# Cross-attention and a mixture of experts: token tiles in groups inside the last attention turns, the token list built from lanes, outputs back in 2 KB rows

## Reference

```python
x = x + attn(layernorm(x), ctx, ctx, mask, Wq, bq, Wk, bk, Wv, bv, Wo, bo)
flat = layernorm(x).reshape(-1, 256)                      # 1792 rows
probs = softmax(flat @ router_w)                          # 8 experts
topk_w, topk_idx = top_k(probs, 2); topk_w /= topk_w.sum(-1)
h = silu(einsum('td,edf->etf', flat, w1))                 # 256 -> 512
y = einsum('etf,efd->etd', h, w2)                         # 512 -> 256
x = x + sum of topk_w * y over a token's two experts
```

## Time and profile before

| | |
|---|---|
| median of 3 executions | 522.26 us (521.93 to 522.46) |
| profiled execution, its own time | 520.47 us |
| its span, first to last instruction | 518.3 us |
| mean granted TensorE clock | 0.896 of 2.4 GHz |
| busy: PE, DVE, ACT, POOL | 424.2 (82%), 348.9 (67%), 262.6 (51%), 189.3 (37%) us |
| chain that ended last | PE 74%, DVE 9%, issue 5%, DMA 4%, ACT 4% |
| moved by DMA | 70.08 MB, mean 135 GB/s; fullest slice 393 GB/s |

### The profile page before, as it was taken

How to read it: one execution, slowest core, us unless ns; L and a number is a source line. 1 busy time by engine, 2 the same in 40 slices (tenths; PEclk the granted TensorE clock), 3 DMA queues, 4 the chain that set the end, 5 groups by cost and what they waited for, 6 DMA issues and landing times.

```text
span 518.3 us, 10586 instructions
## 1 busy us (share of the span) xinstructions
PE 424.2 (82%) x4151; PEld 391.1 (75%) x4151; DVE 348.9 (67%) x743; ACT 262.6 (51%) x338; POOL 189.3 (37%) x162
## 2 busy tenths in 40 slices
PE   2666689999999999999996758445799999999800
PEld 2454489999999999999885657345799999999800
DVE  2776557788788788877871296474667667777427
ACT  3230245666666566666555204101877777777500
POOL 8270462222222222222100430007277777776410
PEclk9796779999999999999999687655999999999965
DMA  7949658676666677775604398002022222221158
GB/s 179 220 145 282 181 149 161 136 143 148 134 146 136 147 152 151 151 151 124 122 4 145 103 393 307 10 1 81 32 82 83 92 82 90 84 91 63 52 166 289
DMA packets 60609, 70.08 MB, mean 135 GB/s; under 512 B 19313, under 2 KB 55681, under 8 KB 60561
## 3 DMA queue, kind: packets, MB, share of 16 engines
q1 hardware_dynamic: 48224, 48.18, 39.8%
q0 software_dynamic: 4032, 11.02, 6.3%
q10 hardware_dynamic: 8304, 10.23, 5.6%
HBM read 35.64 MB, written 15.04 MB: 98 GB/s over the span
## 4 chain that ended last, share of the span: by engine, by line
PE 74%; DVE 9%; issue 5%; DMA 4%; ACT 4%; POOL 2%; SPq 1%; POOLq 0%; DVEq 0%; ACTq 0%
PE ps L1268 39%; PE ps L1329 11%; PE ps L1344 9%; PE ps L1358 8%; PE ps L1558 2%; ACT probs L678 2%; DMA y_back<-y_rows 2%; PE ps L1371 1%; SPq L477 1%; DVE x_rows_sb L927 1%; PE ps L1548 1%; DVE neg_max L880 1%; PE ps L1508 1%; DVE stats L916 1%; PE ps L1381 1%
## 5 line engine op out<-in xcount | busy, mean ns | idle before, releaser
L880 DVE TENSOR_REDUCE neg_max<-ps 112x1 f32<-112x376 f32 x256 | 133.7, 545 | 39.1 <-PE ps L1329 34.0
L678 ACT ACTIVATE probs<-ps 125x1344 f32<-125x1344 f32 x64 | 82.7, 1292 | 42.4 <-PE ps L1344 36.5
L1329 PE MATMUL ps<-k_stack,q_stack 98*112 98x376 f32 x256 | 89.2, 383 | 10.1 <-issue 6.0
L508 POOL TENSOR_TENSOR k_lo<-k_f,k_hi 128x752 fp32r<-128x752 f32 x16 | 28.8, 1802 | 139.2 <-ACT k_hi L652 136.7
L617 POOL DMA_INDIRECT y_rows<-y_out,slot_of_row x42 | 53.2, 1266 | 37.2 <-ACT y_out L814 30.8
L609 POOL DMA_INDIRECT rows<-xn_rows,token_of_row x42 | 42.9, 1021 | 61.2 <-DVE token_of_row L1142 47.5
L1329 PEld LDWEIGHTS ps<-k_stack,q_stack 98*112 98x112 f32 x256 | 45.7, 181 | 24.1 <-DVE neg_max L880 13.4
L1344 PE MATMUL ps<-q_stack,k_stack 100*125 100x224 f32 x384 | 53.6, 276 | 3.3 <-ACT probs L678 3.0
L1344 PEld LDWEIGHTS ps<-q_stack,k_stack 100*125 100x125 f32 x384 | 51.2, 191 | 5.1 <-ACT probs L678 4.9
L1268 PE MATMUL ps<-w_hi,h_hi 128*128 128x256 f32 x168 | 49.0, 292 | 3.1 <-issue 1.6
L1268 PE MATMUL ps<-flat_t_hi,w_hi 128*128 128x256 f32 x168 | 48.8, 290 | 2.8 <-DVE flat_t_lo L1179 2.8
(11 more groups left out here) (189 smaller groups left out, 974.1 us busy)
## 6 DMA issues: line engine op xcount, KB each, us to landing
k_stack<-k_hi SPq DMA_DIRECT2D x64, 188.0 KB, 4.5
w_all<-w ACTq DMA_DIRECT2D x16, 512.0 KB, 8.4
k_stack<-k_lo SPq DMA_DIRECT2D x32, 188.0 KB, 5.4
ctx_raw<-ctx_t SPq DMA_DIRECT2D x32, 187.5 KB, 5.1
q_stack<-q_scratch SPq DMA_DIRECT2D x32, 168.0 KB
q_scratch<-q_hi SPq DMA_DIRECT2D x16, 224.0 KB, 3.1
y_back<-y_rows SPq DMA_DIRECT2D x14, 256.0 KB, 5.5
q_scratch<-q_lo SPq DMA_DIRECT2D x8, 224.0 KB, 2.9
```

What stands on the lines that cost most here:

```text
L508: pool.tensor_tensor(kl[:, :, :], kf[:, :, :], kh[:, :, :].bitcast(F32), ALU.subtract)\
L678: act.activation(pf[j % 2][:, :, :], ps[0:CT, BK_ST:BK_ST + KT, 0:4 * S], ACT.Exp).then_inc(pf_ready, 1)
L880: dve.tensor_reduce(neg_max[:, s:s + 1], ps[0:S, BK_MAX + s % 2, 0:CP], AX.X, ALU.max, negate=True).then_inc(max_read, 1)
L1329: pe.matmul(ps[0:S, BK_MAX + a, 0:CP], qs[b.ring][0:R_MAX, q, S * a:S * (a + 1)], ks[b.ring][0:R_MAX, q, :], start=True, stop=True).then_i ...
```

## The change

Token tiles are taken in units: six units of two tiles and two of one (`UNITS`). `project_output` of units 0 to 3 takes the place of the keys in turns 13 and 14, on PE, and `residual` that on DVE. x is loaded into `x2` ahead of SP's turn 10; POOL makes its constants and all seven bias adds after its turn 12, ahead of `key_low(15)`. The last batch's turn is written out on each engine, with units 4 to 7, transposes, routes and reads of logits woven in. Statistics and roots are taken in groups of 8, 4, 1 and 1 tiles: the first two by a power on POOL, which also normalises those tiles; the last two by Newton steps on DVE. The router's product is turned round: token tiles are stationary, 8 columns move, and the logits need no way back. The choice of experts, ranking and places are made for tiles 0 to 11 and then for tiles 12 and 13. The list: every expert has 14 lanes of 128 places, a place's lane doesn't depend on the other experts' counts, POOL writes each token's slot number in its lane (`lanes`), PE adds them up in 28 products (`fill_lanes`) and one product brings the lanes that are used to the blocks (`list_rows`). Spare rows read one row of zeros. `y_rows` keeps a token's two outputs side by side, so they come back in seven pieces of 512 KB. `weigh` comes after expert step 3. The weights are loaded by SP in two pieces, w1 after the last quad scores and w2 after the last `out_copy`, with the write-out of units 4 and 5 between and of 6 and 7 behind. Many buffers get other places in memory.

```diff
+UNITS = ((0, 2), (2, 2), (4, 2), (6, 2), (8, 2), (10, 2), (12, 1), (13, 1))
+GROUPS = ((0, 4), (4, 2), (6, 1), (7, 1))
+EARLY_NT = 12
...
@@ SP
             for b in range(B):
+                if b == 10:
+                    sp.wait_ge(qproj_done, 2 * NG)
+                    sp.dma_start(x2[:, :, :], x_tiles.rearrange("n p d -> p n d")).then_inc(x2_in, 16)
                 turn(Batch(0, b))
...
+            for u in range(0, 4):
+                write_rows(u)
+            sp.wait_ge(st_done, QUADS * B)
+            sp.dma_start(w1_all[:, :, :].rearrange("p e (k n) -> p (e k) n", k=KD),
+                         w1.rearrange("e k p n -> p (e k) n")).then_inc(w1_in, 16)
+            for u in range(4, 6):
+                write_rows(u)
+            sp.wait_ge(ot_ready, B)
...
+            for u in range(6, 8):
+                write_rows(u)
...
-                for c in range(TOP):
-                    sp.dma_start(y_back[c][:, 2 * g:2 * g + 2, :],
-                                 y_rows[c * T + g * TG:c * T + (g + 1) * TG, :].rearrange("(n p) d -> p n d", p=P))\
-                        .then_inc(y_in[g], 16)
+                sp.dma_start(y_back[:, 2 * g:2 * g + 2, :, :],
+                             y_rows[TOP + TOP * TG * g:TOP + TOP * TG * (g + 1), :]
+                             .rearrange("(n p c) d -> p n c d", p=P, c=TOP)).then_inc(y_in[g], 16)
@@ POOL
+            def roots(g):
...
+                pool.wait_ge(row_var_ready, g + 1)
+                pool.tensor_tensor(row_rstd[:, tiles], row_var[:, tiles], minus_half[:, tiles], ALU.pow)\
+                    .then_inc(row_rstd_ready, 1)
+            def normalise_rows(u):
+                pool.wait_ge(row_rstd_ready, 1 if u < 4 else 2)
+                if u >= RINGS:
+                    pool.wait_ge(ft_done, u - RINGS + 1)
+                    pool.wait_ge(xn_written[u % RINGS], 16)
...
+            def lanes(tiles, known):
+                pool.wait_ge(lanes_known, known)
+                for c in range(TOP):
+                    for n in range(tiles.start, tiles.stop):
+                        last = pool.tensor_scalar(placed[:, c, n, :], place_no[:, 0:ER], lane_of[:, c, n:n + 1],
+                                                  slot_no[:, c, n:n + 1], ALU.is_equal, ALU.mult)
+                last.then_inc(lanes_ready, 1)
+            for b in range(B + 1):
+                turn(Batch(0, b))
+                if b == B - 4:
+                    pool.wait_ge(x2_in, 16)
+                    pool.wait_ge(vo_bias_in, 16)
+                    constants()
+                    for g in range(NT // 2):
+                        add_bias(g)
+            roots(0)
+            for u in range(0, 4):
+                normalise_rows(u)
+            roots(1)
+            for u in range(4, 6):
+                normalise_rows(u)
+            lanes(slice(0, EARLY_NT), 1)
+            lanes(slice(EARLY_NT, NT), 2)
@@ ACT, last turn
+            out_copy(last.after(-1))
+            exps(last, 0)
+            exps(last, 1)
+            attn_high(last.after(-1))
+            exps(last, 2)
+            flat_high(0)
+            exps(last, 3)
+            flat_high(1)
+            flat_high(2)
+            out_copy(last)
+            flat_high(3)
+            flat_high(4)
+            attn_high(last)
+            flat_high(5)
...
@@ DVE: from row_vars(2) on
+            residual(6)
+            row_vars(2, row_stats(6))
+            normalise(last)
+            flat_low(3)
+            read_logits(3)
+            flat_low(4)
+            attn_low(last)
+            read_logits(4)
+            flat_low(5)
+            normalise_late(6)
+            read_logits(5)
+            residual(7)
+            row_vars(3, row_stats(7))
+            flat_low(6)
+            find_two(early_tiles, 6)
+            count_early()
+            normalise_late(7)
+            read_logits(6)
+            flat_low(7)
+            place_rows(early_tiles, BK_RANK, 1)
+            read_logits(7)
+            find_two(late_tiles, 8)
+            for c in range(TOP):
+                places_in_block(c, early_tiles)
+            place_rows(late_tiles, BK_LATE, 2)
+            for c in range(TOP):
+                places_in_block(c, late_tiles)
+            count_blocks()
+            blocks_of_lanes()
+            read_lanes()
+            list_tokens()
             plan_steps()
-            weigh()
             for n in range(-1, STEPS + 1):
                 expert_step(Batch(0, n))
+                if n == 3:
+                    weigh()
@@ PE
+            def route(u):
+                pe.wait_ge(fl_ready, u + 1)
+                for a in range(UNITS[u][1]):
+                    m = slice(a * P, (a + 1) * P)
+                    last = product(ps[:, BK_FLAT[u % 2], E * a:E * (a + 1)],
+                                   [(x[u % 2][:, k, m], w[:, k, :]) for k in range(KD)
+                                    for x, w in ((fh, rwh), (fh, rwl), (fl, rwh))])
+                last.then_inc(logits_done, 1)
...
+                    elif halves[-1] == KD - 1:
+                        project_output(2 * (b.n - B + 3) + t)
...
+            quad_outputs(last.after(-1), 2)
+            quad_outputs(last.after(-1), 3)
+            quad_scores(last, 0)
+            project_output(4)
+            out_transpose(last.after(-1))
+            quad_scores(last, 1)
+            quad_outputs(last, 0)
+            project_output(5)
+            attn_transpose(last.after(-1))
+            quad_scores(last, 2)
+            flat_transpose(0)
+            quad_outputs(last, 1)
+            flat_transpose(1)
+            quad_scores(last, 3)
+            route(0)
+            flat_transpose(2)
+            quad_outputs(last, 2)
+            route(1)
+            flat_transpose(3)
+            quad_outputs(last, 3)
+            project_output(6)
+            route(2)
+            flat_transpose(4)
+            out_transpose(last)
+            route(3)
+            flat_transpose(5)
+            attn_transpose(last)
+            route(4)
+            flat_transpose(6)
+            route(5)
+            project_output(7)
+            route(6)
+            rank_early()
+            flat_transpose(7)
+            route(7)
+            fill_lanes(slice(0, EARLY_NT))
+            rank_late()
+            fill_lanes(slice(EARLY_NT, NT))
             list_rows()
```

More of the change, by code:

```diff
@@ L146, in xattn_moe_kernel @@
         cursor["at"] = shared
+        x2 = sb("x2", [P, NT, D])
+        assert cursor["at"] <= q_end, "x2 lies where the transposed rows were"
+        cursor["at"] = q_end
+        attn_start = cursor["at"]
         expert_even = expert_buffers(0)
-        cursor["at"] = max(q_end, cursor["at"])
-        attn_start = cursor["at"]
+        late_start, cursor["at"] = cursor["at"], attn_start
+        placed = sb("placed", [P, TOP, NT, ER], F32R)
+        assert cursor["at"] <= attn_start + 6 * KD * CP * 4, "lanes lie where the context's parts were"
+        cursor["at"] = attn_start
         c_raw = [sb(f"ctx_raw{p}", [P, KD, CP]) for p in range(2)]
@@ L204, in xattn_moe_kernel @@
         assert cursor["at"] <= hidden_end, "the hidden rows lie where the transposed attention was"
-        cursor["at"] = hidden_at
-        is_place = sb("is_place", [P, TOP, NT, P], F32R)
-        is_its_block = sb("is_its_block", [P, TOP, NT, NB])
-        block_token = sb("block_token", [P, TOP, NT, NB], F32R)
-        assert cursor["at"] <= hidden_end, "the lists are made where the hidden rows come"
-        cursor["at"] = attn_start + 4 * NT * D
-        y_back = [sb(f"y_back{c}", [P, NT, D]) for c in range(TOP)]
+        cursor["at"] = late_start
@@ L238, in xattn_moe_kernel @@
+        is_place = sb("is_place", [P, TOP, NT, P], F32R)
+        assert cursor["at"] <= last_ring_end, "places lie where the last ring was"
+        cursor["at"] = last_ring_end
+        ones = sb("ones", [P, P], F32R)
+        earlier = sb("earlier", [P, P], F32R)
+        block_of_lane = sb("block_of_lane", [P, NB], F32R)
+        lane_tokens = sb("lane_tokens", [P, P], F32R)
+        slot_i = sb("slot_of_row", [P, NB], I32)
+        token_i = sb("token_of_row", [P, NB], I32)
         st2 = sb("stats2", [P, NT, 6])
@@ L988, in turn @@
                     keys(b.after(3), 0)
+                else:
+                    residual(2 * (b.n - B + 3) + 0)
                 if has(after):
@@ L992, in turn @@
                     keys(b.after(3), 1)
+                else:
+                    residual(2 * (b.n - B + 3) + 1)
                 if has(after):
@@ L1080, in find_second, with wide2 @@
-            def find_second():
-                step(dve.scalar_tensor_tensor(out=rest[:, :, :], in0=picked, scalar=-3.0e38,
-                                              in1=logits[:, :, :], op0=ALU.mult, op1=ALU.add))
-                step(dve.tensor_reduce(c2[:, :], rest[:, :, :], AX.X, ALU.max))
-                first_of(rest[:, :, :], c2, second)
-                dve.wait_ge(tri_set, 1)
```

(15 more changed lines are left out.)

640 lines of the change are left out of this document (333 added, 307 removed).

## The result

The changed kernel takes 544.07 us (median of 4 runs, 539.94 to 545.76) against 522.1 us before; two further executions of it took 537.50 and 542.70. The ratio, 1.038 with a 95% interval of 1.031 to 1.045, is taken from the means of all six and of the four before, without the longest of the six, which counts as a slow run. Forecast were 525.0 us and a range of 515 to 533: the direction was right, the size far off. The profiled execution took 539.94 us (span 538.1), before's 520.47 (span 518.3).

The account below looks back on a forecast made before the run. A serial chain from output projections to the first expert matmul (292.20 to 356.50 us) was taken as the bound. List +2.5 (including the earlier turns), weigh +1.2, rows back -1.0 gave +2.7: 522.26 to 525.0 us, range 515 to 533.

Parts of the forecast that it names:

- Part 1: Projections of tiles 0 to 7 in turns 13 and 14: +1.8 us a turn, +3.6 for both (0 to 5.7).
- Part 3: Constants and seven bias adds on POOL before the last key_low: +0.2 us, from 0 to 2.
- Part 2: Load of x, 1.8 MB, in turn 10 ahead of stacking batch 12's keys: +0.5 us, from 0 to 3.
- Part 4: Tail from last attention to the list, 24 POOL lanes at 0.30 us each: list complete +2.5 us (-1.9 to +3.8).
- the second rival: The rival "POOL sets the pace".
- POOL sets the pace: Tail: lanes at 0.46 (+3.8) and POOL standing still during DVE's comparisons (3.4): 532.2 us; chance 0.15.
- The clock stays up: Rival: the tail keeps PE at 2.4 GHz, 11.3 us less, 513.7 us, or 519.3 for half of that; chance 0.30.
- Part 5: Weigh in the fourth expert step, 3.1 us of delay on DVE: +1.2 us, from 0 to 1.8.
- Part 6: Outputs read back at the kernel's end in 2 KB rows, seven loads for fourteen: -1.0 us (-2.1 to 0).
- The power: Roots by power on POOL, no row to price it: hidden up to 3 us, at 4 costing 0.3.

Follow-up runs that it names:

- The pieces: Changed kernel with x loaded in seven pieces of two tiles, one ahead of each of turns 4 to 10, not one 1.8 MB load: 539.09 us.
- the load behind the stackings: Changed kernel with the single 1.8 MB load of x still in turn 10 but issued behind the stacking of batch 12: 544.17 us.
- with products added for it, and the lanes split: Changed kernel, x in pieces, power roots, late ranking and weights first, early lanes shared by DVE and POOL, plus unread products on PE: 509.8 us (515.61 without).
- the first set of added products: Changed kernel, x in pieces, all lanes on DVE, power roots, late ranking and weights first, plus 237 unread 256-column products on PE: 519.13 us (516.64 without).
- lanes on DVE: Changed kernel with all 28 lanes written on DVE and none on POOL: 536.25 us.
- places held: Changed kernel with DVE making the early places only once POOL's 24 early lanes are done: 545.28 us.
- powers: Changed kernel with the roots of the last two tiles taken by one power each on POOL, not 15 steps on DVE: 542.4 us.

## Why the prediction was wrong

**Part 1 was right.** 1.8 us for turn 13 and 3.6 for both. Part 3 was right: key_low of batch 15 started at 265.20 and its stacking at 267.03, as much behind the forecast as the turns were, and no PE wait followed.

**Part 2 failed at "+0.5, from 0 to 3".** The argument was that part of the load falls into a pause of the queue and the keys have some slack. Whatever stands behind the transfer comes 4 us late, and the price is not the wait alone: 4.3 us of wait and 2.5 of half clock behind it, in all 6.8 in the changed kernel's trace, and 2.6 to 4.7 in the others. The pieces and the load behind the stackings settle it for this place in the kernel: within a turn it is the size of the one transfer, not its order among the stackings. In the kernel before the same load, after the last values, holds nothing up, so a place outside the urgent traffic is a remedy too, but too late for this change.

**Part 4 failed at "I take 0.30, nearer the row that also has two operations".** The lane costs 0.73 us. The bounds were 0.22 and 0.46, so even the interval was wrong; by the working stated, 0.1 fixed and the rest by length, the upper one is 0.41. Both rows that made them are of 16 partitions and constants as scalars, one writing bytes; the lane has 128 partitions and two scalars read from a column for each. The nearest form in the trace after, 256 columns at 1.23, lies with 0.73 for 112 on a line of 0.34 us fixed and 3.4 ns a column; no form before had both. The 24 lanes took 20.45 us in place of 7.2: 24 x 0.43 = 10.3 from the price, 3.1 from POOL standing still, which stood in the second rival and beside the sum but not in it. The late lanes add 2.0 (3.17 for 1.2). The rest of the walk was priced 2 us too high, 1.2 of it ahead of the lanes, where PE's clock was still 1.00 up to 311; together the 13.3 us of the table (88.0 for 74.7).

**The rivals.** "POOL sets the pace" was what happened, in its mechanism: lanes longer than DVE's work beside them, and a POOL that stands still for DVE's comparisons (3.4 forecast, 3.1 measured). It had a chance of 0.15 and the lane at 0.46, and gave 532.2; with 0.73 it would have given 538.7, and the load of x comes on top. The chance did not fit the forecast's own numbers: the rival was to decide as soon as 24 lanes take longer than 6.5 us, and the sum already had them at 7.2. "The clock stays up" did not happen by itself; with products added for it, and the lanes split, it gave 5.8 us; the first set of added products gave nothing in the median.

**Part 5** (+1.2) measured +1.9, just over its bound of 1.8: DVE had less room in a step than read. **Part 6** (-1.0) measured -1.7, and 2.3 when undone. The expert steps otherwise came 3.2 us shorter: the clock was up again some 3 us after the first product, where before it took 6, and the products of the rows with w1 took 277 ns each in place of 282 (groups between 392 and 490 us of both traces). That term was not in the sum.

**The power** was priced "hidden up to 3 us". It took 1.68 and 1.03 us for its two groups on POOL, which is within that. What the forecast took over from the change unexamined was that the last two roots belong on DVE; one power takes 0.56 us on POOL in place of 2.9 on DVE.

What stays open: why TensorE's clock falls at 292 to 300 beside a busy engine, and why the traces with lanes on DVE, places held and powers have expert steps 4 to 6 us longer than the changed kernel's.

## What to carry to other kernels

A small instruction that is to be repeated dozens of times on the critical path is priced by a row of its own form (partitions, per-partition scalars, output type), and where the trace has none, the range must say so: two rows of another form bounded this one wrongly by a factor of 1.6. A large load on a queue that also carries small urgent transfers goes out in pieces no longer than the slack of whatever is behind it, or where nothing urgent follows; moving it behind the first urgent transfer only held up the next one here. And work that is spread thin over the end of a dense phase may lose more by TensorE's clock than it gains by overlap, so read the granted clock of the new stretch before the busy times.

## What was not expected of the hardware

- POOL: tensor_scalar with two column scalars, 128x112: 0.731 us, 128x256: 1.226; on DVE the 112 columns go at a pitch of 0.25. A power of 1, 4, 8 columns: 0.56, 1.03, 1.68 us, 0.16 a column.
- One POOL instruction stood still for 3.1 us while DVE ran two comparisons of 1536 elements with two inputs; the DVE instructions themselves took 1.75 us each, as without POOL beside them (1.75 when they were held back until the lanes were done).
- 7 KB behind a load of 1.8 MB on one queue landed after 6.4 us.
- The granted clock fell to 0.50 at 295 with PE busy 8.6 of the 10 us before. In ten traces without added products it fell at 292 to 300, in one at 311; in the two with wide products added in the waits at 309 and 311, for 10 and 7 us only.
